# Gated cross attention and FFN on one core: one weighting block a sequence, wide turned maxima, new engine orders, bias added in the queries stage

## What is computed

```python
q, k, v = norm(x) @ Wq, ctx @ Wk, ctx @ Wv          # 16 heads of 16; 112 queries, 375 keys a sequence
scores = where(mask == 0, -1e9, q @ k.T / sqrt(16))
x = x + tanh(g) * (softmax(scores) @ v @ Wo + bo)   # then x = x + tanh(g') * ffn(norm(x))
```

## Time and profile before

| | before |
|---|---|
| median of 3 runs | 1952.69 us |
| the profiled execution: its time, its span | 1951.86 us, 1949.9 us |
| PE busy (weight loads apart) | 1614.2 us, 83% |
| DVE / ACT / POOL busy | 1075.8 / 831.8 / 859.0 us |
| first key row of attention 0 to last output store | 114.9 to 664.7 us |
| the same of attention 1 | 1099.2 to 1650.8 us |
| mean granted PE clock | 0.936 of 2.4 GHz |

### The profile page before, as it was taken

How to read it: one execution, slowest core, us unless ns; L and a number is a source line. 1 busy time by engine, 2 the same in 40 slices (tenths; PEclk the granted TensorE clock), 3 DMA queues, 4 the chain that set the end, 5 groups by cost and what they waited for, 6 DMA issues and landing times. The chain is left out here.

```text
span 1949.9 us, 40780 instructions
## 1 busy us (share of the span) xinstructions
PE 1614.2 (83%) x15271; PEld 1055.9 (54%) x15271; DVE 1075.8 (55%) x3491; ACT 831.8 (43%) x1822; POOL 859.0 (44%) x842
## 2 busy tenths in 40 slices
PE   1659999999999599999967499999999997706997
PEld 1336666666666355556643256666666664604875
DVE  4646666656666355545536366666666664533653
ACT  3335555555555322222213255555555554213442
POOL 0057766666666300000000466667666665053432
PEclk9879999999999899999989599999999999557999
DMA  7544344334443211211215444444444441225540
GB/s 203 171 75 80 78 84 86 83 81 83 86 86 66 57 53 56 61 54 57 73 50 170 86 98 102 99 94 92 99 101 99 96 91 27 76 77 152 165 131 26
DMA packets 217955, 175.40 MB, mean 90 GB/s; under 512 B 70058, under 2 KB 211311, under 8 KB 217768
## 3 DMA queue, kind: packets, MB, share of 16 engines
q1 hardware_dynamic: 212136, 163.13, 35.6%
q0 software_dynamic: 5632, 9.78, 1.6%
HBM read 99.53 MB, written 41.15 MB: 72 GB/s over the span
## 5 line engine op out<-in xcount | busy, mean ns | idle before, releaser
L902 ACT ACTIVATE probs_a<-bank 125x448 f32<-125x448 f32 x768 | 410.6, 538 | 183.5 <-PE bank L782 182.5
L752 PE MATMUL bank<-k_stack_a,q_stack_a 96*128 96x375 f16 x1024 | 315.0, 329 | 72.3 <-DVE row_max_a L952 38.0
L656 POOL TENSOR_TENSOR probs_a<-probs_a,keep_a 125x448 int32<-125x448 int32 x256 | 289.5, 1133 | 147.9 <-ACT probs_a L902 145.8
L656 POOL TENSOR_TENSOR probs_a<-probs_a,mask_keep 125x448 int32<-125x448 int32 x256 | 289.6, 1133 | 146.9 <-ACT probs_a L902 144.7
L952 DVE CUSTOM_DVE_ANT_0 masked_scores_a<-bank,mask_add 112x375 bf16<-112x375 f32 x512 | 269.1, 546 | 148.6 <-PE bank L752 147.0
L952 DVE CUSTOM_DVE_ANT_0 masked_scores_a<-bank,mask_add_a 112x375 bf16<-112x375 f32 x512 | 269.1, 546 | 147.5 <-PE bank L752 144.5
L782 PE MATMUL bank<-q_stack_a,k_stack_a 97*128 97x224 f16 x1536 | 274.1, 260 | 0.1
L664 POOL TENSOR_TENSOR ctx_low_a<-ctx_in_a,ctx_high_a 128x375 f16<-128x375 f32 x128 | 114.8, 898 | 244.3 <-ACT ctx_high_a L875 243.2
L799 PE MATMUL bank<-probs_a,values_a 125*32 125x112 f32 x6144 | 200.4, 263 | 10.4 <-POOL probs_a L656 1.4
L1251 PE MATMUL bank<-h0h_f,ffn_w 128*128 128x448 f16 x512 | 180.6, 353 | 12.0 <-DVE h0l_f L1130 11.9
L799 PEld LDWEIGHTS bank<-probs_a,values_a 125*32 125x32 f32 x6144 | 140.2, 109 | 75.9 <-issue 73.8
(11 more groups left out here) (199 smaller groups left out, 3083.2 us busy)
## 6 DMA issues: line engine op xcount, KB each, us to landing
ctx_in_a<-in_ctx_dram SPq DMA_DIRECT2D x64, 375.0 KB, 4.0
k_stack_a<-k_high_a SPq DMA_DIRECT2D x256, 93.8 KB, 3.8
w_in_e<-in_L_ffn_W_dram SPq DMA_DIRECT2D x16, 1024.0 KB, 8.0
k_stack_a<-k_low_a SPq DMA_DIRECT2D x128, 93.8 KB, 3.9
q_stack_a<-q_split SPq DMA_DIRECT2D x128, 84.0 KB, 3.4
q_split<-high_q SPq DMA_DIRECT2D x32, 224.0 KB, 3.2
mask_in_f<-in_mask_BxSxS_if_dram SPq DMA_DIRECT2D x8, 656.2 KB, 6.6
mask_keep<-keep_f SPq DMA_DIRECT2D x8, 656.2 KB
```

The costliest lines, as they stand in the source:

```text
L656: pool.tensor_tensor(bits, bits, cols, ALU.mult).then_inc(masked, 1)
L752: pe.matmul(ring(row_use(h))[:, 0:S2], q_stack[x.four][0:STACK, at:at + P], k_stack[x.four][0:STACK, (h // 2) * S2:(h // 2 + 1) * S2], sta ...
L902: act.activation(probs[:, i, :], score_bank[i % 3][0:CK, 0:GT], ACT.Exp, scale=DK ** -0.5).then_inc(exped, 1)
```

## The change

In the attention stage: `weigh` does all twelve units at the end of a step, with one count of `weighted` a sequence in place of four. `max_parts` becomes 112 x 2 x 128, zero past the 8 columns, and the turn takes all 128 columns, so the weights that it loads are as wide as those of its neighbours. The order of PE, ACT, DVE and POOL in a step is written anew; rows 0 and 1 of sequence p are now made late in the step that makes p's keys, and the ring's order is a table (`RING`). The key DMAs go half by half. POOL's mask units come first, then both context parts. `x_old` and `base` go: SP loads `x_sum` directly, once the store of two sequences back has landed, from a new DRAM tensor `based`, x plus bias, which POOL makes in the queries stage and SP stores.

```diff
# queries_phase
+        xb = [sb(f"xb{n}", [S, G, D], F32) for n in range(2)]
...
-                    wait(sp, xn_ready, s.back(2).value + 1 if s.back(2).exists(NG) else 0)
+                    hold(sp, xn_ready, s.back(2).value + 1 if s.back(2).exists(NG) else 0, passed)
+                    hold(sp, xb_ready, s.back(2).value + 1 if s.back(2).exists(NG) else 0, passed)
                     sp.dma_start(xg[s.slot][:, :, :], take(x_rows, s.value)).then_inc(x_loaded[s.slot], 16)
+                w = s.back(1)
+                if w.exists(NG):
+                    hold(sp, xb_ready, w.value + 1, passed)
+                    sp.dma_start(take(xb_rows, w.value), xb[w.slot][:, :, :]).then_inc(xb_stored[w.slot], 16)
...
+                    pool.tensor_tensor(xb[s.slot][:, :, :], xg[s.slot][:, :, :],
+                                       m["bo"][layer][:, :].unsqueeze(1).to_broadcast([S, G, D]), ALU.add).then_inc(xb_ready, 1)
# attention_phase
+RING = ((2, 2), (3, "second"), (2, 3), (2, 4), (2, 5), (2, 6), (2, 7), (2, 8), (2, 9), (2, 10), (2, 11), (2, 12),
+        (1, 0), (2, "first"), (2, 13), (2, 14), (1, 1), (2, 15))
-        max_parts = sb("max_parts", [S, H], F16)
+        max_parts = sb("max_parts", [S, 2, P], F16)
...
+        ring = [(s - back, what) for s in range(B + 4) for back, what in RING if 0 <= s - back < B]
+        def wait_bank(pe, n, what):
+            at = use_of[n.value, what]
+            if at >= 3:
+                before = ring[at - 3]
...
# SP
-                    wait(sp, based, d.back(2).value + 1 if d.back(2).exists(B) else 0)
-                    sp.dma_start(x_old[d.two][:, :], take(x_in, d.value)).then_inc(x_loaded[d.two], 16)
+                    wait(sp, x_stored[d.two], 16 * d.use2)
+                    sp.dma_start(x_sum[d.two][:, :], take(x_in, d.value)).then_inc(x_loaded[d.two], 16)
...
+                    for n in range(2):
+                        for g, tile, ready in ((0, k_high, k_high_ready), (2, k_high, k_high_ready),
+                                               (1, k_low, k_low_ready)):
# POOL
-                for i in range(UNITS):
-                    if d.exists(B) and i in pool_units:
+                for i in pool_units:
+                    if d.exists(B):
                         mask_unit(d, i)
-                    if s.exists(B) and i in (2, 8):
-                        low_context(s, i // 8)
-                    if d.exists(B) and i == 5:
-                        base(d)
+                if s.exists(B):
+                    low_context(s, 0)
+                    low_context(s, 1)
# PE
-                pe.transpose(dst, max_parts[:, HH * half:HH * (half + 1)], ident_h[0:S, 0:S]).then_inc(max_turned, 1)
+                pe.transpose(dst, max_parts[:, half, :], ident_h[0:S, 0:S]).then_inc(max_turned, 1)
-            def weigh(n, group):
-                for i in range(CH * group, CH * (group + 1)):
+            def weigh(d):
+                for i in range(UNITS):
```

More of the change, by code:

```diff
@@ L303, in queries_phase @@
         stored = [sem(f"stored{n}") for n in range(2)]
+        xb_ready, xb_stored = sem("xb_ready"), [sem(f"xb_stored{n}") for n in range(2)]
         passed = sem("passed")
@@ L579, in q_view, with bank_of @@
             return q_stack[slot][:, 0:NP * 2 * S].rearrange("w (p t) -> w p t", p=NP)
[L581 to L591, removed]
+        ring = [(s - back, what) for s in range(B + 4) for back, what in RING if 0 <= s - back < B]
+        use_of = {use: at for at, use in enumerate(ring)}
+        rows = [use for use in ring if isinstance(use[1], int)]
+        row_count = {row: at + 1 for at, row in enumerate(rows)}
+        def bank_of(n, what):
+            return row_bank[use_of[n.value, what] % 3]
+        def wait_bank(pe, n, what):
+            at = use_of[n.value, what]
+            if at >= 3:
+                before = ring[at - 3]
+                if before in row_count:
+                    pe.wait_ge(rows_maxed, row_count[before])
+                else:
+                    pe.wait_ge(max_ready, 2 * before[0] + 1 + (before[1] == "second"))
         @block.sync
@@ L740, in score_row @@
                     pe.wait_ge(k_loaded[x.two], 96 * (x.use2 + 1))
[L742 to L750, removed]
+                wait_bank(pe, x, h)
                 at = (h // 2) * 2 * S + (h % 2) * S
-                pe.matmul(ring(row_use(h))[:, 0:S2], q_stack[x.four][0:STACK, at:at + P],
+                pe.matmul(bank_of(x, h)[:, 0:S2], q_stack[x.four][0:STACK, at:at + P],
                           k_stack[x.four][0:STACK, (h // 2) * S2:(h // 2 + 1) * S2],
@@ new lines, in units, with rows @@
+                def units(*numbers):
+                    for i in numbers:
+                        if d.exists(B):
+                            score_unit(d, i)
+                def rows(*numbers):
+                    for h in numbers:
+                        if x.exists(B):
+                            score_row(x, h)
+                units(0)
+                rows(2)
+                if p.exists(B):
+                    make_keys(p, x, d, e, 0)
+                if d.exists(B):
+                    turn_maxima(d, 1)
@@ new lines, in body @@
+                rows(3)
+                units(1)
+                rows(4)
+                units(2, 3)
+                rows(5, 6)
+                units(4)
+                if p.exists(B):
+                    make_keys(p, x, d, e, 1)
+                rows(7, 8)
+                units(5)
+                rows(9)
+                if e.exists(B):
+                    turn_heads(e)
+                units(6, 7)
+                if x.exists(B):
+                    make_values(x, p, e, (2,))
+                rows(10)
@@ new lines, in body @@
+                units(8)
+                if e.exists(B):
+                    turn_heads_back(e)
+                units(9)
+                rows(11)
+                if x.exists(B):
+                    make_values(x, p, e, (0, 1))
+                rows(12)
+                units(10)
+                if p.exists(B):
+                    score_row(p, 0)
+                if x.exists(B):
+                    turn_maxima(x, 0)
+                units(11)
+                rows(13)
+                if e.exists(B):
+                    project(e, x)
@@ L865, in _ @@
+                rows(14)
+                if p.exists(B):
+                    score_row(p, 1)
+                rows(15)
+                if d.exists(B):
+                    weigh(d)
             run_quads(B, 4, body)
@@ new lines, in units @@
+                def units(*numbers):
+                    for i in numbers:
+                        if d.exists(B):
+                            weigh_up(d, e, i)
+                if e.exists(B):
+                    act.wait_ge(weighted, e.value + 1)
+                    wait(act, heads_turned, e.value)
+                    act.activation(heads_t[:, :], head_bank[:, 0:GT], ACT.Copy).then_inc(heads_ready, 1)
+                units(0)
+                if p.exists(B):
+                    high_keys(p, 0)
@@ new lines, in body @@
+                if d.exists(B):
+                    copy_maxima(d, 1)
+                units(1, 2, 3, 4)
+                if s.exists(B):
+                    split_context(s, 0)
+                if p.exists(B):
+                    high_keys(p, 1)
+                if s.exists(B):
+                    split_context(s, 1)
+                units(5, 6, 7)
+                if x.exists(B):
+                    copy_values(x, e, (2,))
+                units(8)
+                if e.exists(B):
+                    act.wait_ge(turned_back, e.value + 1)
+                    wait(act, projected, e.value)
+                    act.activation(heads_n[:, :, :], head_bank[:, 0:KC * S].rearrange("p (c t) -> p c t", c=KC),
+                                   ACT.Copy).then_inc(back_ready, 1)
@@ L938, in _ @@
         def _(dve):
+            dve.memset(max_parts[:, :, HH:], 0.0)
             for n in range(4):
```

216 lines of the change are left out of this document (92 added, 124 removed).

## The result

The changed kernel takes 1960.58 us, the median of 20 runs (1949.88 to 1982.61), against 1951.44 (1948.27 to 1954.39) for the kernel before: a ratio of 1.0046, 95% interval 1.0032 to 1.006. The forecast was 1887 us and a range up to 1945; it came out slower, by a little.

What follows compares the result with a forecast made beforehand. PE's in-order program was taken as the bound, at 16.84 us a step; 58 steps at -1.25 us (-72.5), ramps +5 and queries +2 gave -65.5, so 1887 us, range 1835 to 1945.

Steps and rivals of the forecast that it cites:

- hidden by 0.4: SP's queue in attention: loop from output store to landed keys takes 15.2 us in layer 1, under the 15.6 us step.
- the walk of the ring and the keys: One attention step followed from its first unit: PE's waits for ring banks and key transfers stay at 1.9 us.
- One block: Weighting at the step's end: 96 records with one shape change, 2.5 us against 3.24, so -0.8 us a step.
- Wide tile: Turn of the maxima: loading 128 columns saves 0.19 us a turn, 0.38 us a step.
- So row 4 ... starts at 2.66 and row 6 waits for its bank until 3.26: Ring in attention: row 4 queues on DVE behind the keys' low part, so PE waits 0.65 us at row 6.
- the waits at rows 9 and 10: Ring in attention: PE waits 0.3 us for a bank at row 9 and 0.45 us at row 10.
- rival B: Ring waits go too, the walk being too strict: 13.8 us a step, about 1783 us; chance 0.06.
- A wait of 0.45: Row 0 of p, late in the step: PE waits 0.45 us for the last key transfer, starting at 10.85.
- Rival C: SP's queue becomes the bound through slow output-store landings: loop 17.5 us in layer 1, about 1974 us; chance 0.10.
- Rival D: New waits eat the shape gain, the walk missing 1.2 us of them: 1952 us or a little above; chance 0.07.
- +1 us a layer: Queries stage: POOL's bias sums and their stores cost 1 us a layer, between nothing and 23.
- Ramps +5: Start of each attention stage: first rows stand behind the second sequence's key transfers, some 2.5 us a layer.

Runs made afterwards that it cites:

- experiment 4: The kernel before with only the wide tile of maxima (turn taking 128 columns) added: 1930.13 us, ratio 0.9893.
- experiment 2: The changed kernel with rows 0 and 1 put back in the sequence's own step, as first rows of the ring around unit 0: 1880.15 us, ratio 0.963.
- the second execution: A second profiled execution of the changed kernel, with nothing altered: 1961.13 us; that rerun measured 1964.96 us, ratio 1.0077.
- experiment 8: The changed kernel with rows 0 and 1 in their own step, SP's order turned, bias as before with POOL's sum first in its step: 1798.33 us, ratio 0.9213.
- experiment 3: The changed kernel with the bias part undone: queries stage as before, POOL summing x_old and bias between mask units: 1999.06 us, ratio 1.0232.
- experiment 6: The changed kernel with rows 0 and 1 in their own step and SP's order context, second maxima, keys, masks, queries, x: 1820.24 us, ratio 0.932.
- experiment 10: The changed kernel with eight zero-tile stores a layer in the queries stages and no POOL sums, bias left out: 1940.72 us, ratio 0.9926.

## Why the prediction was wrong, point by point

Between the forecast -65.5 and the +9.2 of the ledger lie 75 us: 54 in attention 1, 21 in the queries stages, 13 in attention 0, and 14 the other way in the ramps and ends. The step that failed most is the one on SP, which held the second maxima for 0.75 us on the way, "hidden by 0.4"; next come the price of POOL's sums in the queries stages, and the walk of the ring and the keys.

- **One block: right.** 2.5 us forecast, 2.53 found in the step shown, against 3.24; its worth was not tried alone. **Wide tile: right**, -0.39 us a step against -0.38 (experiment 4). The 128-column load of the turn took 97 ns in the changed kernel and lay under the matmul before it; the 13 us that the prediction worked out by the rule of the Trainium skill, TensorE: Matmul & The Clock Gate, section "LDWEIGHTS (loading the stationary operand)", did not show.
- **"So row 4 ... starts at 2.66 and row 6 waits for its bank until 3.26": wrong.** The ring has three banks, and the diff says `before = ring[at - 3]`; I freed row 6's bank by row 4, two uses back, where it is row 3, which DVE had finished at 402.3 when PE came for row 6 at 402.6. The same slip made the waits at rows 9 and 10. So 1.4 us of waits a step never were, and rival B, "the walk being too strict", was right about them; "three banks" stood in my argument against it. This slip made the forecast too slow, not too fast.
- **"A wait of 0.45" for the keys: mis-sized**, 2.60 in the step shown, 1.8 in the mean. The row was reached 1.02 us earlier (9.38 against 10.4: 1.4 of ring waits gone, 0.3 for the maxima come), and could start 1.13 later: last issue at 6.93 for 6.55, landing in 5.0 for 4.2. A wait for a transfer of the same step takes whatever else is saved ahead of it: in attention 0 the 28 steps lie 28 x (16.02 - 14.17) = 51.8 us above the step of experiment 2, and the waits for keys and maxima there add up to 51.3. That attention 0 came near the forecast, 16.02 against 15.6, is luck, two errors against each other.
- **SP "hidden by 0.4": wrong place.** I followed SP's loop through the keys and took the second maxima only as 0.75 us on the way. They have a consumer of their own, units 6 and 7, 3.3 us after their issue, and they stood right behind masks and queries. The sum asked whether SP's loop fits into a step, and never when each transfer is read. Rival C had SP's queue as the bound, at another transfer; its condition, a slow landing of the output stores, isn't what happened (1.9 us in the median, as before). Rival D named the time best, 1952 or a little above: new waits of PE that the walk missed. Its 1.2 us a step are about what the steps exceed 15.6 by in the mean of both layers (0.42 and 1.87), but since 1.4 us of ring waits fell away, the missed waits are larger. In attention 1 the steps lie 28 x (17.47 - 14.17) = 92.4 us above those of experiment 2's attention 0: 40.4 are waits for maxima, 31.7 for keys in the second execution, which leaves 20. That these are the lower clock (0.94 against 1.00) is an estimate by subtraction; the single fp16 matmuls at the lower level, 112 of them, account for 14.
- **Queries "+1 us a layer": mis-sized, 11.** I asked whether POOL was idle and the stage streamed on PE. While POOL's sum ran, a normalisation of 0.41 us lasted up to 2.5. The upper bound of 23 held it, the chosen value didn't.
- **Ramps +5: not there.** From first context load to first output store it is +0.2 and -2.4 us; the other -6.6 lie behind the 28 steps and at the end.
- The forecast rested on waits found over a step of some 60 instructions. Three of them, each under 0.7 us, made up 1.4 us, more than the whole gain of 1.25. The sum had no margin for one slip in that walk, and the range of 1 us a step did not hold it.

What the engine orders and the shape changes are worth once nothing gives it back is seen in experiment 8, which drops the bias part, keeps rows 0 and 1 in their own step and turns SP's order: 156 us under the kernel before in the same comparison, 1954.56 - 1798.33. Of its 16.84 - 14.17 = 2.67 us a step some 1.2 are the two shape terms of the forecast; the other 1.5 are waits, which the forecast left as they were.

## What to carry to other kernels

When a step's order is rewritten, list each transfer with its issue, what was issued just ahead of it, and its first reader: one that is made and read in the same step swallows all that is saved before it, and a small urgent one belongs ahead of large ones that are wanted a step later. Count a ring's bank back by its full depth. Before work goes to an idle engine, look at which instructions of other engines it will lie beside, not only at its own idle time.

## What the hardware showed that I had not expected

- **POOL and DVE shut each other out.** A normalisation of 0.41 us took up to 2.5 beside a 2.35 us sum, and in experiment 3 a shift of 0.16 us took 3.92, to the end of four POOL instructions in an unbroken run. The Trainium skill, SBUF — State Buffer, section "Who interferes with whom", says that DVE instructions which can run in a two-port mode, tensor_scalar among them, and a GpSimd instruction lock each other out for the whole of an instruction. The trace agrees (both DVE instructions are TENSOR_SCALAR; no run shows the mode) and goes further: in experiment 3 DVE did not get its turn between back-to-back POOL instructions.
- **PE can come back slower from a stand.** Behind eleven of 17 stands for maxima it ran at 1.2 GHz for some us (records of 256 columns 0.42 us long against 0.27), so that a wait can cost more than its length: some 20 us in attention 1, by the estimate above. The length of the stand alone doesn't decide it: 2.01 us at 1339.03 brought the lower level, 2.49 at 1282.06 didn't, and in the second execution attention 0 kept a mean of 0.98 with 27 waits for keys of up to 2.7 us.
- **A 1.8 KB transfer takes longer behind larger ones.** From issue to reader it was 3.3 us at 402.22 and 5.15 at 1333.88, and with masks and queries moved behind it (experiment 6) the wait went. Key transfers, alike in size, took 4.2 for the first and 5.0 for the last of six in one step.
- **SP's issue of a transfer is not a constant.** Two stores of the queries' high part took up to 2.2 us to issue in the queries stage with the bias stores and 0.9 to 1.0 before; experiment 10 has the same 2.1 and lost nothing by it.
